# A fused attention and spectral kernel: one weighing of the last attention groups in another bank and behind its phase, one subtraction in two halves, the last image stored in two tiles

## The chip, the cores and the metric

The kernel runs on one core of one Trainium2 chip. A core has TensorE (PE, matrix products into eight banks of accumulator memory), VectorE (DVE), ScalarE (ACT), GpSimd (POOL) and SyncE (SP, which here only issues transfers). The metric is the device time of one execution in microseconds. Before the change three runs took 353.43, 353.55 and 356.92 us; the median is 353.55.

## The reference

Four layers act on x of 4 images, 16 by 16 places, 192 channels, all in float32:

```
x = x + proj(attention(layernorm(x)));  x = x + fc2(gelu(fc1(layernorm(x))))   # layers 0 and 2
x = irfft2(softshrink(mlp(rfft2(x)))) + x                                      # layer 1
x = dht(shrink(mlp(dht(x)))) / size + x                                        # layer 3
```

Attention has 12 heads of 16 channels in windows of 14 by 14 places. 16 is padded to 28, so each image has one full window and three partly filled ones. Each score gets a bias from the row and column distance, then a softmax over the window's keys, and the probabilities weigh the values. Layer 3 is a Hartley transform over images, places and channels, block-diagonal products, and the transform back.

## The kernel before

One program holds an instruction list for each engine, written out by hand. Semaphores order the engines against each other. Every engine works strictly through its own list.

**Attention** (run twice, `attention(l)`, l = 0 and 1) goes through 18 groups, n = 0 to 17. A group is four heads (a slot) of one image's full window or of the edge windows of all images. Groups 14 to 17 are the third slot of images 0 to 3. A group passes through these steps:

- `score` on PE (L910): queries times keys. For groups 2 to 17 it runs in two halves, each half into two banks: part 0 of group n (half-step h = 2n) into banks 0 and 1, part 1 (h = 2n + 1) into banks 2 and 3.
- `take_max` on DVE (L1461): the negated row maximum out of these banks. Then a transpose, and SP moves the maxima by four small transfers (L664) to where `turn` reads them.
- `turn` on PE (L938): the scores once more, keys by queries and less the maximum, into banks 4 to 7. It has two pairs of heads, 8 products each at an image group's full window. Every product is shown in the trace as two records.
- exponentials on ACT (L1294): one for each bank 4 to 7, into a ring of two buffers.
- `weigh` on PE (L957): probabilities times values and ones, 8 products into one bank. `weighed_in(n)` names it: bank 4 for most groups, and 2, 3 and 7 for groups 15, 16 and 17. Bank 4 is also where `turn` of the next group has put scores, so weighing group n in bank 4 waits until the first exponential of group n + 1 has been read.
- `take_weighed` on ACT (L1281): copies the weighed values out, `invert` on DVE (L1484 to L1490) turns and inverts the sums, `divide` on POOL (L723 for the third slot) divides.
- `out_project` on PE (L801): the output product of an image, once its four groups are divided. Image 0 goes to bank 0.

The main loop works three groups at once: `turn` of group n, `score` of groups n + 2 and n + 3, `weigh` of group n - 1. In the loop of n = 15 the last scores (h = 35, group 17) stand between the products of the first pair. Its second pair has no scores beside it: there the order is half of pair 1, the weighing of group 14, the other half of pair 1. ACT follows with exponentials of pair 0, `take_weighed(14)`, exponentials of pair 1. Then come `turn(16)`, `weigh(15)`, `out_project(0)`, `turn(17)`, `weigh(16)`, `out_project(1)`, `weigh(17)`. `turn(16)` waits for all four exponentials of group 15.

**The last stage** (`spectral3`) starts on DVE with sums and differences of the folded images. The difference of images 0 and 1 against 2 and 3 is one instruction over 776 elements (L1574); it releases PE's first two products (`mix` 3 and 2) at once. PE takes mix 3, 2, 0, 1 in turn (L1135), each 4 products.

**The end**: for the images in the order 1, 3, 0, 2, PE transforms back (L1213), 6 products an image for two tiles of 128 places, into one bank. DVE scales and adds x (L1634), and SP stores the image (L670). SP's last wait is for all stores.

```
return {N_GROUPS - 3: 2, N_GROUPS - 2: 3, N_GROUPS - 1: 7}.get(n, 4)      # weighed_in
```

The functions that the change touches:

## Time and profile before

| | |
|---|---|
| median of three runs | 353.55 us (353.43 to 356.92) |
| the profiled execution | 356.79 us |
| its span, first to last instruction | 354.9 us |
| TensorE busy | 338.2 us (95%) |
| VectorE / ScalarE / GpSimd busy | 203.5 / 144.5 / 98.9 us |
| TensorE share of the chain that ended last | 87% |
| mean granted TensorE clock | 0.99 |

The time beside the span is 1.9 us of start and end. The busy shares say who works most over the whole span, but not who is waited for in a given stretch. For that one follows the chain of waits, in order of time, to the places where TensorE itself sat idle, and reads there what ended the idle time. The profiled execution is 3.24 us longer than the median, so its own numbers must be set against its own time.

### The profile page before, as it was taken

The page shows a single profiled execution, that of the slowest core. Times are in us where ns is not written, and L with a number is a line of the kernel's source. Part 1 is how long each engine was busy: PE and PEld are TensorE (multiplying, and loading weights), DVE is VectorE, ACT ScalarE, POOL GpSimd, SP SyncE. Part 2 cuts the span into 40 slices and gives each one's busy share as a digit, 9 for nine tenths or more (in the row PEclk, how much of TensorE's full clock was granted, in tenths as well). Part 3 has the DMA queues.
Part 4 walks back from the last instruction along what each step waited for, and adds up shares of the span by engine and source line. Part 5 has one row for each costly group of instructions (what it writes and reads, how often), then busy time and mean ns, then how long its engine had stood idle before and what let it go on. Part 6 is the DMA issues. An engine that isn't in the chain of part 4 may idle for free.

```text
span 354.9 us, 10541 instructions
## 1 busy us (share of the span) xinstructions
PE 338.2 (95%) x4462; PEld 259.9 (73%) x4462; DVE 203.5 (57%) x483; ACT 144.5 (41%) x322; POOL 98.9 (28%) x186
## 2 busy tenths in 40 slices
PE   5999999999989999999999999999998899999996
PEld 3459698889966447977846878878886643998576
DVE  6455668777766700126765667777785750135472
ACT  2175155555546352023037415555545452202330
POOL 4000507985311029300000050998431204000000
PEclk9699999999999999999999999999999999999999
DMA  6972000000002003010020100000000000000002
GB/s 210 394 252 60 11 10 15 10 5 4 3 17 109 22 1 113 0 66 2 0 90 16 41 3 14 10 9 5 5 4 5 0 0 2 0 2 0 2 0 89
DMA packets 9888, 14.22 MB, mean 40 GB/s; under 512 B 3505, under 2 KB 7441, under 8 KB 9842
## 3 DMA queue, kind: packets, MB, share of 16 engines
q1 hardware_dynamic: 9794, 13.55, 11.8%
q8 instruction: 35, 0.57, 0.7%
q14 instruction: 11, 0.09, 0.1%
q10 hardware_dynamic: 48, 0.00, 0.0%
HBM read 11.30 MB, written 0.79 MB: 34 GB/s over the span
## 4 chain that ended last, share of the span: by engine, by line
PE 87%; DVE 9%; issue 1%; SPq 1%; ACT 1%; DMA 1%; DVEq 0%
PE banks L938 18%; PE banks L910 12%; PE banks L1030 9%; PE banks L1048 9%; PE banks L957 8%; PE banks L867 6%; PE banks L830 4%; PE banks L801 2%; PE banks L790 2%; PE banks L1213 2%; PE banks L1061 2%; PE banks L1108 2%; PE banks L1078 1%; PE banks L1135 1%; PE banks L1161 1%
## 5 line engine op out<-in xcount | busy, mean ns | idle before, releaser
L1294 ACT ACTIVATE arena<-banks 128x392 f32<-128x392 f32 (+2 forms) x144 | 62.5, 486 | 51.2 <-PE banks L938 51.2
L910 PE MATMUL banks<-attention_arena 32*128 32x196 f32 x384 | 49.4, 357 | 0.9 <-ACT v_and_ones L1270 0.4
L938 PE MATMUL banks<-attention_arena 32*128 32x196 f32 x384 | 47.6, 343 | 2.0 <-ACT arena L1294 2.0
L1461 DVE TENSOR_REDUCE negmax<-banks 128x4 f32<-128x784 f32 x40 | 39.0, 975 | 15.8 <-PE banks L910 15.4
L938 PE MATMUL banks<-attention_arena,keys 32*128 32x196 f32 x384 | 44.3, 323 | 0.0
L910 PE MATMUL banks<-keys,attention_arena 32*128 32x196 f32 x384 | 44.0, 323 | 0.0
L938 PEld LDWEIGHTS banks<-attention_arena 32*128 32x128 f32 x384 | 30.1, 183 | 9.0 <-issue 5.8
L1030 PE MATMUL banks<-yT,fc 128*128 128x512 f32 (+1 forms) x96 | 33.3, 607 | 0.3
L1048 PEld LDWEIGHTS banks<-fc,arena 128*128 128x128 f32 x192 | 31.1, 190 | 1.5 <-ACT arena L1308 1.5
L938 PEld LDWEIGHTS banks<-attention_arena,keys 32*128 32x128 f32 x384 | 32.1, 184 | 0.0
L1048 PE MATMUL banks<-fc,arena 128*128 128x192 f32 x192 | 31.7, 327 | 0.0
L910 PEld LDWEIGHTS banks<-keys,attention_arena 32*128 32x128 f32 x384 | 31.5, 184 | 0.0
L1518 DVE TENSOR_TENSOR x_tok<-banks,x_plus_bias 128x384 f32<-128x384 f32 x8 | 4.5, 558 | 46.2 <-PE banks L1048 46.2
L957 PE MATMUL banks<-arena,v_and_ones 128*32 128x196 f32 (+2 forms) x672 | 30.9, 307 | 0.1
L910 PEld LDWEIGHTS banks<-attention_arena 32*128 32x128 f32 x384 | 27.9, 183 | 3.6 <-DVE negmax L1458 1.9
L938 PE MATMUL banks<-edge_rel,edge_keys 32*128 32x112 f32 (+1 forms) x288 | 29.6, 278 | 0.0
L938 PE MATMUL banks<-edge_q,edge_k 32*128 32x112 f32 (+1 forms) x288 | 28.7, 274 | 0.0
L688 POOL COPY edge_rel<-attention_arena 128x112 f32<-128x112 f32 x6 | 1.4, 280 | 91.2 <-DVE attention_arena L1448 91.2
L1030 PEld LDWEIGHTS banks<-yT,fc 128*128 128x128 f32 (+1 forms) x96 | 12.8, 188 | 18.3 <-issue 16.3
L725 POOL TENSOR_TENSOR divided_part<-o_and_sums,inverse_sums 128x196 f32<-128x196 f32 (+2 forms) x24 | 13.1, 546 | 46.5 <-DVE inverse_sums L1490 46.3
L938 PEld LDWEIGHTS banks<-edge_rel,edge_keys 32*128 32x128 f32 x288 | 22.6, 186 | 2.5 <-issue 2.5
L957 PEld LDWEIGHTS banks<-arena,v_and_ones 128*32 128x32 f32 x672 | 16.8, 109 | 10.1 <-ACT arena L1294 6.6
(168 smaller groups left out, 654.6 us busy)
## 6 DMA issues: line engine op xcount, KB each, us to landing
fc<-in_fc SPq DMA_DIRECT2D x2, 768.0 KB, 5.4
qkv<-in_qkv SPq DMA_DIRECT2D x2, 576.0 KB, 4.5
fc<-in_fc SPq DMA_DIRECT2D x2, 576.0 KB, 5.5
attention_arena<-negmaxT SPq DMA_DIRECT2D x68, 1.0 KB
rel<-in_rel SPq DMA_DIRECT2D x2, 448.0 KB, 5.1
x_tok<-in_x SPq DMA_DIRECT2D x4, 192.0 KB, 3.1
inverse<-in_inverse SPq DMA_DIRECT2D x1, 768.0 KB
edge_rel<-negmaxT SPq DMA_DIRECT2D x48, 0.5 KB
```

The source lines that it names most:

```text
L725: pool.tensor_tensor(part, o, shape(m.inverse[:, ring]), ALU.mult).then_inc(s.divided, 1)
L790: last = nc.tensor.transpose(m.bank[bank0 + 2 * g + half][:, 128 * i:128 * (i + 1)], m.xn[:, 4 * g + i, REST * half:REST * half + 128], c[ ...
L801: last = mm(m.bank[out_bank(b)][:, CH * tile:CH * (tile + 1)], m.oT[:, part, at:at + 128], wl["proj"][:, part], start=part == 0, stop=part ...
L830: ins = mm(bank[:, :], wl["qkv"][rows, half, 128 * g:128 * (g + 1)], m.yT[rows, half, 512 * part:512 * (part + 1)], start=not short, stop= ...
L867: ins = mm(bank[row(quad), 192 * n:192 * (n + 1)], wl["rel"][row(quad), 0 if kind == "rel_h" else 1, at % WIN], q[:, :, :, at], start=True ...
L910: ins = mm(o, asking, asked, start=not with_rel, stop=bool(with_rel))
L938: last = mm(m.bank[4 + j][:, cols * tile:cols * (tile + 1)], keys_of(slot, b, j, tile)[with_rel], queries_of(slot, b, j)[with_rel], start= ...
L957: last = mm(m.bank[weighed_in(n)][row(j), 0:cols], values_of(slot, b, j, tile), m.probsT[:, n % P_RING, j, cols * tile:cols * (tile + 1)], ...
L1030: ins = mm(m.bank[j % 8][:, :], wl["fc1"][rows, half, 128 * hid:128 * (hid + 1)], m.yT[rows, half, 512 * g:512 * (g + 1)], start=not short ...
L1048: last = mm(m.bank[4 + b][:, CH * tile:CH * (tile + 1)], m.hidT[:, hid, at:at + 128], wl["fc2"][:, hid], start=hid == 0, stop=hid == HID_T ...
L1294: run(m.probsT[:, n % P_RING, j, 0:cols], m.bank[4 + j][:, 0:cols], ACT.Exp).then_inc(s.probs, 1)
L1461: dve.tensor_reduce(at[:, 4 * part:4 * part + 4].rearrange("k (j a) -> k j a", a=2), m.banks[:, 2 * part:2 * part + 2, 0:2 * MAIN_KEYS].re ...
```

## The change

Four things change.

1. Group 14 is weighed into bank 0 instead of bank 4. So it waits no longer for an exponential of group 15's own bank, but for the maximum of h = 34, the last that reads bank 0. `turn` of groups 16 and 17 waits for one copy-out less (`pv_out` 14 instead of 15), and `out_project(0)`, which uses bank 0, waits for the copy-out of group 14.
2. In the loop of n = 15 (`last_scored`), `weigh(14)` stands behind all of `turn(15)`, and `take_weighed(14)` on ACT behind the exponentials of both pairs. This holds in both attention layers.
3. In `spectral3` the 776-element subtraction becomes two of 388 elements, mix 3 first, each with its own release.
4. The last image's two tiles go to banks 4 and 5, are scaled by two DVE instructions of 192 elements, and are stored by two transfers of half the size.

```diff
@@ -309,3 +309,7 @@
 def weighed_in(n):
-    return {N_GROUPS - 3: 2, N_GROUPS - 2: 3, N_GROUPS - 1: 7}.get(n, 4)
+    return {N_GROUPS - 4: 0, N_GROUPS - 3: 2, N_GROUPS - 2: 3, N_GROUPS - 1: 7}.get(n, 4)
+
+
+def last_scored(n):
+    return n + AHEAD + 1 == N_GROUPS
 
@@ -668,5 +672,10 @@
             for n, b in enumerate(OUT_ORDER):
-                sp.wait_ge(S3.inv.dve, n + 1)
-                sp.dma_start(out_dram[b], m.xb[:, b]).then_inc(stored, 16)
-            sp.wait_ge(stored, 16 * IMAGES)
+                if n < IMAGES - 1:
+                    sp.wait_ge(S3.inv.dve, n + 1)
+                    sp.dma_start(out_dram[b], m.xb[:, b]).then_inc(stored, 16)
+                else:
+                    for tile in range(2):
+                        sp.wait_ge(S3.inv.dve, IMAGES + tile)
+                        sp.dma_start(out_dram[b][:, tile], m.xb[:, b, tile]).then_inc(stored, 16)
+            sp.wait_ge(stored, 16 * (IMAGES + 1))
 
@@ -931,3 +940,3 @@
                     if n >= 2:
-                        pe.wait_ge(s.pv_out, min(n - 1, N_GROUPS - 3))
+                        pe.wait_ge(s.pv_out, min(n - 1, N_GROUPS - 4))
                     at, landed = max_landed(n)
@@ -950,3 +959,3 @@
                     pe.wait_ge(s.probs, 4 * (n + 1))
-                    pe.wait_ge(s.max, 2 * N_GROUPS)
+                    pe.wait_ge(s.max, 2 * N_GROUPS - 1 if weighed_in(n) == 0 else 2 * N_GROUPS)
                 cols, tiles = queries(b), key_tiles(b)
@@ -1001,3 +1010,3 @@
                                 score(l, h + 1, quarter(steps_of(h + 1), q))
-                            if q == 1 and n > 0:
+                            if q == (3 if last_scored(n) else 1) and n > 0:
                                 weigh(l, n - 1)
@@ -1009,3 +1018,3 @@
                             if b == 0:
-                                pe.wait_ge(s.max, 2 * N_GROUPS)
+                                pe.wait_ge(s.pv_out, N_GROUPS - 3)
                             out_project(s, wl, b)
@@ -1131,3 +1140,3 @@
                 for n, mix in enumerate((3, 2, 0, 1)):
-                    pe.wait_ge(S3.mixed, {3: 1, 2: 1, 0: 2, 1: 3}[mix])
+                    pe.wait_ge(S3.mixed, n + 1)
                     for part in range(2):
@@ -1212,5 +1221,7 @@
                                 pe.wait_ge(S3.back.act, 3)
-                            last = mm(m.bank[1 + n][:, CH * tile:CH * (tile + 1)], c["space_back"][:, row, 128 * tile:128 * (tile + 1)], gb,
+                            bank = m.bank[IMAGES + tile if n == IMAGES - 1 else 1 + n]
+                            last = mm(bank[:, CH * tile:CH * (tile + 1)], c["space_back"][:, row, 128 * tile:128 * (tile + 1)], gb,
                                       start=i == 0, stop=i == 2)
-                    last.then_inc(S3.inv.pe, 1)
+                        if tile == 1 or n == IMAGES - 1:
+                            last.then_inc(S3.inv.pe, 1)
 
@@ -1294,3 +1305,3 @@
                             run(m.probsT[:, n % P_RING, j, 0:cols], m.bank[4 + j][:, 0:cols], ACT.Exp).then_inc(s.probs, 1)
-                        if n > 0 and pair == 0:
+                        if n > 0 and pair == last_scored(n):
                             take_weighed(n - 1)
@@ -1573,3 +1584,4 @@
                 dve.wait_ge(S3.folded, FOLDED)
-                dve.tensor_tensor(m.mix[:, 2:4], m.folded[:, 0:2], m.folded[:, 2:4], ALU.subtract).then_inc(S3.mixed, 1)
+                dve.tensor_tensor(m.mix[:, 3], m.folded[:, 1], m.folded[:, 3], ALU.subtract).then_inc(S3.mixed, 1)
+                dve.tensor_tensor(m.mix[:, 2], m.folded[:, 0], m.folded[:, 2], ALU.subtract).then_inc(S3.mixed, 1)
                 dve.tensor_tensor(m.ef[:], m.folded[:, 0:2], m.folded[:, 2:4], ALU.add).then_inc(S3.ef, 1)
@@ -1632,5 +1644,11 @@
                 for n, b in enumerate(OUT_ORDER):
-                    dve.wait_ge(S3.inv.pe, n + 1)
-                    dve.scalar_tensor_tensor(m.xb[:, b], m.bank[1 + n][:, 0:2 * CH].rearrange("k (t c) -> k t c", t=2),
-                                             1.0 / (TOKENS * CH), m.x[:, b], ALU.mult, ALU.add).then_inc(S3.inv.dve, 1)
+                    if n < IMAGES - 1:
+                        dve.wait_ge(S3.inv.pe, n + 1)
+                        dve.scalar_tensor_tensor(m.xb[:, b], m.bank[1 + n][:, 0:2 * CH].rearrange("k (t c) -> k t c", t=2),
+                                                 1.0 / (TOKENS * CH), m.x[:, b], ALU.mult, ALU.add).then_inc(S3.inv.dve, 1)
+                        continue
+                    for tile in range(2):
+                        dve.wait_ge(S3.inv.pe, IMAGES + tile)
+                        dve.scalar_tensor_tensor(m.xb[:, b, tile], m.bank[IMAGES + tile][:, CH * tile:CH * (tile + 1)],
+                                                 1.0 / (TOKENS * CH), m.x[:, b, tile], ALU.mult, ALU.add).then_inc(S3.inv.dve, 1)
```

The lists of the two kernels, first TensorE's, second attention layer. The rows from the second pair of `turn(15)` to the first product of `out_project(0)`. "L957" and "L966" are `weigh`, "L938" and "L947" are `turn`; [waits ...] names the semaphores: `probs` counts exponentials, `max` maxima, `pv_out` copy-outs, `weighed` divisions. Before:

```order
L938 MATMUL banks<-attention_arena 128x196 [waits max_rows1_0,pv_out1,probs1]
L938 MATMUL banks<-attention_arena 128x196
L938 MATMUL banks<-attention_arena,keys 128x196 x2
L957 MATMUL banks<-arena,v_and_ones 32x196 [waits probs1]
L957 MATMUL banks<-arena,v_and_ones 32x196 x7
L938 MATMUL banks<-attention_arena 128x196 x2
L938 MATMUL banks<-attention_arena,keys 128x196 x2
L938 MATMUL banks<-attention_arena 128x196 [waits max_rows1_1,pv_out1,probs1]
```

After:

```order
L947 MATMUL banks<-attention_arena 128x196 [waits max_rows1_0,pv_out1,probs1]
L947 MATMUL banks<-attention_arena 128x196
L947 MATMUL banks<-attention_arena,keys 128x196 x2
L947 MATMUL banks<-attention_arena 128x196 x2
L947 MATMUL banks<-attention_arena,keys 128x196 x2
L966 MATMUL banks<-arena,v_and_ones 32x196 [waits max1,probs1]
L966 MATMUL banks<-arena,v_and_ones 32x196 x7
L947 MATMUL banks<-attention_arena 128x196 [waits max_rows1_1,pv_out1,probs1]
```

The 8 products of the weighing moved behind the second half of `turn(15)`; its wait now names `max` too.

ScalarE's list at the same place, from the exponentials of group 15's first pair to those of group 16's first pair ("L1281" and "L1292" are `take_weighed`, "L1294" and "L1305" the exponentials). Before:

```order
L1294 ACTIVATE arena<-banks 128x392 [waits pv1,turned1_0]
L1294 ACTIVATE arena<-banks 128x392
L1281 ACTIVATE o_and_sums<-banks 128x196 [waits weighed1,pv1]
L1294 ACTIVATE arena<-banks 128x392 [waits turned1_1]
L1294 ACTIVATE arena<-banks 128x392
L1294 ACTIVATE arena<-banks 128x392 [waits pv1,turned1_0]
```

After:

```order
L1305 ACTIVATE arena<-banks 128x392 [waits pv1,turned1_0]
L1305 ACTIVATE arena<-banks 128x392
L1305 ACTIVATE arena<-banks 128x392 [waits turned1_1]
L1305 ACTIVATE arena<-banks 128x392
L1292 ACTIVATE o_and_sums<-banks 128x196 [waits weighed1,pv1]
L1305 ACTIVATE arena<-banks 128x392 [waits pv1,turned1_0]
```

The copy-out moved behind the second pair's exponentials.

## Rows read from the trace of the kernel before

**Rows 1.** Chain of waits, second attention layer: start, duration in us, work, record count

```profile
268.21 0.80 PE banks L957 x16
269.01 0.91 PE banks L938 x8
...
270.89 1.61 PE banks L938 x32
...
273.31 1.50 PE banks L801 x8
```

**Rows 2.** Timeline, same stretch: start, duration, instructions, [idle before <-releaser]

```profile
267.58 0.89 ACT L1294 ACTIVATE arena<-banks 128x392 f32<-128x392 f32 x2 [0.45 <-PE banks L938]
269.16 0.33 ACT L1281 ACTIVATE o_and_sums<-banks 128x196 f32<-128x196 f32 x1 [0.69 <-PE banks L957]
269.95 0.89 ACT L1294 ACTIVATE arena<-banks 128x392 f32<-128x392 f32 x2 [0.46 <-PE banks L938]
270.89 0.61 PE L938 MATMUL banks<-attention_arena 32*128 32x196 f32 x8 [1.01 <-ACT arena L1294]
```

**Rows 3.** The same timeline, VectorE, GpSimd and SyncE

```profile
266.33 0.97 DVE L1461 TENSOR_REDUCE negmax<-banks 128x4 f32<-128x784 f32 x1 [0.16 <-PE banks L910]
268.99 2.20 SPq L664 DMA_DIRECT2D attention_arena<-negmaxT  x4
273.81 0.41 DVE L1484 STREAM_TRANSPOSE o_turned<-o_and_sums 128x224 f32<-128x224 f32 x1 [2.91 <-ACT o_and_sums L1281]
274.99 0.61 POOL L723 TENSOR_TENSOR attention_arena<-o_and_sums,inverse_sums 128x196 f32<-128x196 f32 x1 [3.40 <-DVE inverse_sums L1490]
279.50 0.46 PEld L801 LDWEIGHTS banks<-proj,attention_arena 128*128 128x128 f32 x3 [0.43 <-POOL attention_arena L723]
278.83 0.61 POOL L723 TENSOR_TENSOR attention_arena<-o_and_sums,inverse_sums 128x196 f32<-128x196 f32 x1 [3.23 <-DVE inverse_sums L1490]
```

**Rows 4.** Timeline, first attention layer

```profile
104.41 0.61 PE L938 MATMUL banks<-attention_arena 32*128 32x196 f32 x8 [1.01 <-ACT arena L1294]
108.22 0.41 DVE L1490 STREAM_TRANSPOSE inverse_sums<-recip 128x224 f32<-128x224 f32 x1 [0.23 <-DVE recip L1486]
```

**Rows 5.** Timeline, start of the last stage, VectorE and TensorE

```profile
319.78 0.97 DVE L1574 TENSOR_TENSOR arena<-attention_arena 128x776 f32<-128x776 f32 x1
320.66 0.96 DVE L1575 TENSOR_TENSOR arena<-attention_arena 128x776 f32<-128x776 f32 x1
321.65 0.56 DVE L1577 TENSOR_TENSOR arena<-arena 128x388 f32<-128x388 f32 x1
322.14 0.56 DVE L1578 TENSOR_TENSOR arena<-arena 128x388 f32<-128x388 f32 x1
323.98 0.30 DVE L1591 TENSOR_TENSOR arena<-banks,arena 97x144 f32<-97x144 f32 x1
320.80 4.16 PE L1135 MATMUL banks<-space_cas,arena 128*97 128x144 f32 x32 [0.64 <-DVE arena L1574]
```

**Rows 6.** Timeline, end: the last scaling and its store

```profile
351.91 0.56 DVE L1634 SCALAR_TENSOR_TENSOR x_plus_bias<-banks,x_tok 128x384 f32<-128x384 f32 x1 [1.39 <-PE banks L1213]
352.50 0.37 SPq L670 DMA_DIRECT2D out<-x_plus_bias  x1
```

**Rows 7.** Page, issues: KB each, us to landing

```profile
out<-x_plus_bias SPq DMA_DIRECT2D x4, 192.0 KB, 2.0
```

**Rows 8.** Stretches: busy time of five engines, granted clock, transfer share, GB/s

```profile
353.30:353.40 0.10, 0.00 (x0) 0.00 (x0) 0.00 (x0) 0.00 (x0) 0.00 (x0) 1.00 0.11 38
354.00:354.10 0.10, 0.00 (x0) 0.00 (x0) 0.00 (x0) 0.00 (x0) 0.00 (x0) 1.00 0.31 92
9.00:10.00 1.00, 0.75 (x1) 0.50 (x2) 0.97 (x7) 0.00 (x0) 0.00 (x0) 0.50 1.05 358
```

**Rows 9.** Chain of waits, first projection of the kernel

```profile
9.25 5.46 PE banks L830 x6
...
15.92 4.94 PE banks L830 x14
```

## The prediction

> **What bounds the kernel now.** I read the chain of waits first, in order of time. TensorE carries 87% of it, so an instruction of another engine is worth time only where TensorE stands still beside it. The change touches four places, and TensorE stands still at three of them.
>
> In each attention layer the chain leaves TensorE once between groups 15 and 16. In the second layer it runs: `weigh(14)` at 268.21 for 0.80, the second half of `turn(15)` at 269.01 for 0.91, then ScalarE, then `turn(16)` at 270.89 [rows 1]. The timeline shows why: the exponentials of group 15's second pair start at 269.95, 0.03 us after that half, and take 0.89, while TensorE is idle for 1.01 us and is released by them [rows 2]. So the weighing stands in front of the work that ScalarE waits for, and the time behind it is empty. The first layer has the same 1.01 us [rows 4]. At the start of the last stage TensorE idles 0.64 us for one subtraction of 0.97 us [rows 5]. At the end nothing runs beside the last scaling, its store and the landing [rows 6, 7].
>
> **The change part by part.**
>
> *The weighing behind `turn(15)`, twice.* Nothing is added or removed; 0.80 us of TensorE's work moves behind the last products of `turn(15)`. These end at 269.92 - 0.80 = 269.12. ScalarE is free then (its first pair ended at 267.58 + 0.89 = 268.47), and has no copy-out in front any more. It runs from 269.15 to 270.04. `turn(16)` started 0.05 after the exponentials and does so again, at 270.09 instead of 270.89: **0.80 us**. The weighing ends at 269.92 and lies in the gap, of which some 0.2 us is left. Its new wait, the maximum of h = 34, was done at 266.33 + 0.97 = 267.30 [rows 3], so bank 0 is free.
>
> What gets later is the copy-out of group 14: from 269.16 to 270.04. Behind it hang VectorE's inversion, GpSimd's division and `out_project(0)`. The same steps for group 15 take from 273.81 to the end of the division at 274.99 + 0.61 = 275.60, so 1.79 us. The copy takes 0.33 and VectorE starts some 0.03 behind it: 270.40 + 1.79 = 272.19. From a division to TensorE the row of `out_project(2)` shows 279.50 - 279.44 = 0.06 us. So `out_project(0)` is released at 272.25 [rows 2, 3]. TensorE reaches it at 273.31 - 0.80 = 272.51. That is 0.26 us of slack. In the first layer one inversion stood 0.23 us longer between two of its own steps [rows 4]; there the slack is 0.03. I cost this at nothing, and name it as the tightest place.
>
> SyncE's queue isn't touched here, but the small transfers of the maxima now have less time. The last four issues end at 268.99 + 2.20 = 271.19. Even with the 2.0 us of the 192 KB store they land at 273.2, and `turn(17)` needs them at 272.51 + 1.50 = 274.01 [rows 3, 7]. The copy-out wait of `turn` 16 and 17 goes away, but was no row's releaser. Everything behind is released by TensorE, so it moves with it. Two layers: 1.60 us. Bounds: at most the whole idle, 1.01 each; at least 0.4 each, if the division is late.
>
> *The subtraction in halves.* One of 776 elements took 0.97; one of 388 takes 0.56, and the next of a pair starts 0.49 behind the first [rows 5]. TensorE starts 0.05 behind 319.78 + 0.56, at 320.39 instead of 320.80: **0.41 us**. The second half is done at 320.83, needed at 321.43 (each mix takes 4.16/4 = 1.04). VectorE's later work starts 2 x 0.49 - 0.88 = 0.10 later. So mix 0 is ready at 321.65 + 0.56 + 0.10 + 0.05 = 322.36 and needed at 320.39 + 2.08 = 322.47. The last input of the channel products (L1591) is ready at 323.98 + 0.30 + 0.15 = 324.43 and needed at 324.55. Both are covered by TensorE's own products, by only 0.11 us. Without that cover up to 0.1 us is given back; bounds 0.30 to 0.41.
>
> *The last image by tiles.* TensorE ends when it did. The last scaling shrinks from 384 to 192 columns. Between 0.30 for 144 and 0.56 for 384 elements [rows 5, 6], 192 take 0.30 + 48 x 0.26/240 = 0.35: 0.21 us less. The store lands 2.0 us after its issue; its bytes move from about 353.39 to 354.03, 0.64 us [rows 7, 8], of which half goes: 0.32. The first tile's store is issued a microsecond earlier, so its 0.37 of SyncE lies before the second tile is ready. **0.53 us.** For the landing the bounds are 0 (it is all fixed) and 1.0 (it is all proportional); I take 0.32, since the bytes' own time is what the rows show.
>
> The Trainium skill (DMA: Bandwidth & Descriptors, Anatomy of one DMA) fits about 2.0 us plus bytes/436e3, on the GpSimd path. By it the half store saves 0.23 instead of 0.32, and the sum falls by 0.09. Its whole for 192 KB would be 2.45, and the row has 2.0, so the fit is high here; I stay with the rows.
>
> The fourth edit, banks 4 and 5 for the two tiles, costs nothing: bank 5 was last read before the first image's products. The sum is 1.60 + 0.41 + 0.53 = 2.54 us.
>
> **Against which time.** The profiled execution took 356.79, the median 353.55. The difference has a place: from 9 to 15 us TensorE's granted clock is 0.50, its level of 1.2 GHz, after a stretch with idle time before it [rows 8]. Six records of the first projection take 5.46 there, against 14 in 4.94 later at 2.4 GHz, which is 0.353 each [rows 9]. That is 5.46 - 2.12 = 3.34 us, against 3.24 between profile and median. So I take the sum off both: 354.25 for an execution with this fall, 351.0 for one without.
>
> **The rivals.**
>
> *The division becomes the wait.* For it: slacks of 0.26 and 0.03. Against it: eight such divisions of one length. If two steps stand 0.23 longer, as one did, the layers lose 0.20 and 0.43: 351.0 + 0.6 = 351.6, and to 352.2 at the bounds. It decides from 0.26 us on.
>
> *The median falls on executions with the slow stretch.* This is the one that ends above the time before. The place is the first projection, the price 3.3 us, and it decides when more than half of the timed runs have it: 351.0 + 3.3 = 354.3, slower than 353.55 by 0.2%. For it: of four executions shown two have such a time (356.79, 356.92). Against it: the change leaves everything before 100 us as it was, and the median before was free of it. The Trainium skill (TensorE: Matmul & The Clock Gate, What's actually happening) says that the point at which the clock rises differs from run to run of one kernel. The two groups of times agree with that.
>
> *Nothing is won in attention*, because the exponentials were held by something else than the products. The rows name only the products. It would leave 0.94 us: 352.6.
>
> **How the numbers follow.** Forecast 60%, late division 12%, slow stretch 24%, nothing in attention 2%, other 2%. The predicted time is 351.0. The forecast's own range adds up the bounds: a gain of 1.3 gives 352.2, one of 3.1 (most of the idle time and 0.9 at the end) 350.4. The slow stretch must be in, or a quarter is left out, so the range is 350.5 to 354.5. A measurement of this kernel can tell about 1% from no change, which is 3.5 us. Faster by more needs a gain of 3.5, beyond the bounds unless the two kernels' medians fall on different sides of the slow stretch: 6%. Slower by more needs both the stretch and something unforeseen: 2%. Within: 92%.
>
> **What would show it.** `turn(16)` should start 0.2 us behind the end of `weigh(14)`, in both layers, and the 1.01 us of idle time be gone. No wait on GpSimd before `out_project(0)`, or one below 0.1. TensorE's idle before L1135's successor near 0.23, with no new one between the mixes. A last scaling of 0.35 and a landing near 1.7. Wrong would be: an idle TensorE before `out_project(0)` of over 0.3, a wait on VectorE before mix 0 or the channel products, a landing of 2.0 still, or a clock of 0.50 anywhere behind 16 us.

## The result

Eighteen runs of each kernel gave a median of 351.93 us (350.38 to 353.88) for the changed one and 355.23 us (353.34 to 357.27) for the one before. The ratio of the two kernels, which is that of their mean times (352.05 and 355.00), is 0.9917, with a 95% interval of 0.9892 to 0.9942. That is 2.95 us less, with an interval of 2.1 to 3.8; the two medians are 3.30 us apart. Runs that took over 1.5% more than the fastest of the same kernel are left out of the medians, ranges and ratios of this text; among these thirty-six there is none. The prediction was 351.0, in a range of 350.5 to 354.5, with "within 1%" at 92%, and a sum of 2.54 us off. The measured median lies in the range. The three runs that the prediction started from had a median of 353.55; the kernel before is 1.7 us slower than that in the longer series, so the fall of 2.95 is what can be compared with the 2.54, and the median cannot be taken off 353.55.

The changed kernel's page:

```profile
PE 338.1 (96%) x4462; PEld 260.3 (74%) x4462; DVE 204.1 (58%) x485; ACT 144.6 (41%) x322; POOL 99.1 (28%) x186
```

TensorE does the same work (338.1 against 338.2 us) in a span of 351.3 us, which is 3.6 us shorter. The rest of this section finds those 3.6 us.

**The attention groups.** The chain of waits of the changed kernel, second attention layer, as [rows 1]:

```profile
265.82 1.35 PE banks L947 x16
...
267.59 0.50 ACT arena L1305
268.09 0.04 issue
268.13 1.61 PE banks L947 x32
269.74 0.80 PE banks L966 x16
270.54 1.50 PE banks L810 x8
```

The weighing stood as a piece of 0.80 us between two pieces of `turn(15)`. It has left the chain, and the last 16 records of `turn(15)` are one piece of 1.35 us. Before, they were two, of 0.66 and 0.91 us. The first layer shows both:

```profile
101.06 0.66 PE banks L938 x8
101.73 0.80 PE banks L957 x16
102.53 0.91 PE banks L938 x8
```

The timeline of the same stretch, as [rows 2, 3]:

```profile
267.02 0.21 DVE L1487 STREAM_TRANSPOSE negmaxT<-negmax 128x32 f32<-128x32 f32 x1
267.19 0.89 ACT L1305 ACTIVATE arena<-banks 128x392 f32<-128x392 f32 x2 [0.45 <-PE banks L947]
268.10 0.33 ACT L1292 ACTIVATE o_and_sums<-banks 128x196 f32<-128x196 f32 x1
268.13 0.61 PE L947 MATMUL banks<-attention_arena 32*128 32x196 f32 x8 [0.18 <-ACT arena L1305]
269.64 0.61 POOL L732 TENSOR_TENSOR attention_arena<-o_and_sums,inverse_sums 128x196 f32<-128x196 f32 x1 [0.89 <-DVE inverse_sums L1501]
270.47 0.62 PEld L810 LDWEIGHTS banks<-proj,attention_arena 128*128 128x128 f32 x4 [0.31 <-issue]
```

TensorE's idle time before `turn(16)` fell from 1.01 to 0.18 us. The transpose of the last maximum (L1487) hangs on the last scores, ahead of the edit, so it is a good mark to measure from: from it to `turn(16)` are 268.13 - 267.02 = 1.11 us. Its row before:

```profile
268.75 0.21 DVE L1476 STREAM_TRANSPOSE negmaxT<-negmax 128x32 f32<-128x32 f32 x1
```

There it was 270.89 - 268.75 = 2.14. Each layer gained **1.03 us**, not 0.80; the first layer shows the same 1.11 and 2.14.

**The start of the last stage**, timeline and then chain of waits of the changed kernel, as [rows 5]:

```profile
317.02 0.56 DVE L1585 TENSOR_TENSOR arena<-attention_arena 128x388 f32<-128x388 f32 x1
317.50 0.56 DVE L1586 TENSOR_TENSOR arena<-attention_arena 128x388 f32<-128x388 f32 x1
...
321.30 0.30 DVE L1603 TENSOR_TENSOR arena<-banks,arena 97x144 f32<-97x144 f32 x1
317.64 4.16 PE L1144 MATMUL banks<-space_cas,arena 128*97 128x144 f32 x32 [0.24 <-DVE arena L1585]
```

```profile
321.80 4.00 PE banks L1154 x16
```

TensorE waits 0.24 instead of 0.64 us, which is a gain of 0.40. But the next stage (L1154, the channel products) takes 4.00 us. Before it took 3.88:

```profile
324.96 3.88 PE banks L1145 x16
```

So 0.11 to 0.12 us was given back.

**The end**, timeline and issues of the changed kernel, as [rows 6, 7]:

```profile
348.27 1.32 SPq L679 DMA_DIRECT2D out<-x_plus_bias  x2
348.86 0.36 DVE L1652 SCALAR_TENSOR_TENSOR x_plus_bias<-banks,x_tok 128x192 f32<-128x192 f32 x1 [0.62 <-PE banks L1223]
```

```profile
out<-x_plus_bias SPq DMA_DIRECT2D x2, 96.0 KB, 1.6
```

The last scaling takes 0.36 instead of 0.56, the landing 1.6 instead of 2.0. The landings are rounded to 0.1, and so are the spans on the page. The traces hold the spans to the thousandth: 354.878 and 351.277 us. From the first record of the back transform (343.71 and 340.66) to the end that is 11.17 and 10.62: the end gained **0.55 us**, of which 0.20 are the scaling and 0.35 what lies behind it.

The pieces add up: 2 x 1.03 + 0.40 - 0.11 + 0.55 = 2.90 us. The other 0.70 us between the two spans lie before 24 us, where nothing was changed (last part of the experiments): the next stage begins at 24.55 and 23.85. So the 3.60 us are complete. The 2.95 us of the eighteen runs agree with the 2.90, but with an interval of 2.1 to 3.8 they would agree with 2.54 as well.

### The profile page after: what moved, and what is told of

Read it like the earlier page. It is cut to its first block, busy times and chain, and to the rows that moved or that the text cites. A ratio compares the mean times of both kernels' runs of the same rounds, so it can differ in the third digit from the quotient of the medians.

```text
span 351.3 us, 10546 instructions
## 1 busy us (share of the span) xinstructions
PE 338.1 (96%) x4462; PEld 260.3 (74%) x4462; DVE 204.1 (58%) x485; ACT 144.6 (41%) x322; POOL 99.1 (28%) x186
## 4 chain that ended last, share of the span: by engine, by line
PE 87%; DVE 8%; issue 1%; DMA 1%; ACT 1%; SPq 1%; DVEq 0%
PE banks L947 18%; PE banks L919 12%; PE banks L1039 9%; PE banks L1057 9%; PE banks L966 7%; PE banks L876 6%; PE banks L839 4%; PE banks L799 3%; PE banks L810 2%; PE banks L1223 2%; PE banks L1070 2%; PE banks L1117 2%; PE banks L1087 1%; PE banks L1144 1%; PE banks L1170 1%
## 5 line engine op out<-in xcount | busy, mean ns | idle before, releaser
L1305 ACT ACTIVATE arena<-banks 128x392 f32<-128x392 f32 (+2 forms) x144 | 62.5, 486 | 50.5 <-PE banks L947 50.5
L947 PE MATMUL banks<-attention_arena 32*128 32x196 f32 x384 | 47.2, 341 | 0.5 <-ACT arena L1305 0.4
L947 PE MATMUL banks<-attention_arena,keys 32*128 32x196 f32 x384 | 44.3, 323 | 0.0
L947 PEld LDWEIGHTS banks<-attention_arena 32*128 32x128 f32 x384 | 30.2, 183 | 6.8 <-issue 5.1
L947 PEld LDWEIGHTS banks<-attention_arena,keys 32*128 32x128 f32 x384 | 32.1, 184 | 0.0
L966 PE MATMUL banks<-arena,v_and_ones 128*32 128x196 f32 (+2 forms) x672 | 30.9, 307 | 0.1
L947 PE MATMUL banks<-edge_rel,edge_keys 32*128 32x112 f32 (+1 forms) x288 | 29.6, 278 | 0.0
L947 PE MATMUL banks<-edge_q,edge_k 32*128 32x112 f32 (+1 forms) x288 | 28.7, 274 | 0.0
L947 PEld LDWEIGHTS banks<-edge_rel,edge_keys 32*128 32x128 f32 x288 | 22.6, 186 | 2.5 <-issue 2.5
L966 PEld LDWEIGHTS banks<-arena,v_and_ones 128*32 128x32 f32 x672 | 16.8, 109 | 10.1 <-ACT arena L1305 6.2
```

The costliest lines, as they stand in the source:

```text
L947: last = mm(m.bank[4 + j][:, cols * tile:cols * (tile + 1)], keys_of(slot, b, j, tile)[with_rel], queries_of(slot, b, j)[with_rel], start= ...
L966: last = mm(m.bank[weighed_in(n)][row(j), 0:cols], values_of(slot, b, j, tile), m.probsT[:, n % P_RING, j, cols * tile:cols * (tile + 1)], ...
L1305: run(m.probsT[:, n % P_RING, j, 0:cols], m.bank[4 + j][:, 0:cols], ACT.Exp).then_inc(s.probs, 1)
```

## The experiments

I had two theories for the 0.23 us that each attention layer gained above the forecast. S, switching: TensorE loses time whenever it goes from `turn`'s products to a weighing and back. W, waiting: the weighing itself stood waiting for the exponential that frees bank 4. The mark for all kernels is again the transpose of the last maximum:

| kernel | mark to `turn(16)`, layers 1 and 2, us | idle before `turn(16)` | `turn(16)` to `out_project(0)` |
|---|---|---|---|
| before | 2.14, 2.14 | 1.01 | 2.34, 2.35 |
| changed | 1.11, 1.11 | 0.18 | 2.34, 2.34 |
| e1_attention | 1.11, 1.11 | 0.18 | 2.34, 2.34 |
| e4_bank_only | 2.14, 2.14 | 1.01 | 2.34, 2.35 |
| e5_moved_bank4 | 1.50, 1.51 | 0.58 | 2.35, 2.34 |
| e6_act_order | 2.23, 2.23 | 1.31 | 2.35, 3.96 |
| e7_split | 1.11, 1.11 | 0.18, 0.17 | 2.55, 2.56 |
| e9_pool_late | 1.11, 1.11 | 0.18 | 2.55, 2.55 |

The differences are of start times in each kernel's own timeline; the last column goes to the first record of `out_project(0)`. Where a kernel was run once, its whole time is given but not argued from, since single runs of one kernel differ by some 3 us.

**e1_attention** (354.03 us): the kernel before with the attention edits alone.

```diff
-                            if q == 1 and n > 0:
+                            if q == (3 if last_scored(n) else 1) and n > 0:
...
-                        if n > 0 and pair == 0:
+                        if n > 0 and pair == last_scored(n):
```

> The kernel before with the attention edits alone (bank 0, the weighing of group 14 behind all of turn(15), the copy-out behind both pairs). Forecast's sizes: turn(16) starts 0.80 us earlier in each layer and the span is 1.6 us shorter between the same two places. The changed kernel's trace has 1.03 us in each layer. Theory S (switching): a TensorE that goes from turn to weigh and back loses about 0.1 us each way, and the order saves that too: 1.03 us each, 2.06 in both, and the start of the last stage still idles 0.64 us. Theory W (waiting): the 0.23 us above the forecast were a wait of the weighing for the exponential of bank 4.

Measured: 1.03 us in each layer, and 0.64 us of idle time left at the start of the last stage. So the attention edits are worth 2.06 us by themselves.

**e4_bank_only** (355.97 us): the kernel before with group 14 in bank 0, but nothing moved.

```diff
-    return {N_GROUPS - 3: 2, N_GROUPS - 2: 3, N_GROUPS - 1: 7}.get(n, 4)
+    return {N_GROUPS - 4: 0, N_GROUPS - 3: 2, N_GROUPS - 2: 3, N_GROUPS - 1: 7}.get(n, 4)
```

> The kernel before with group 14 weighed in bank 0, but at its old place (in the middle of turn(15)'s second pair) and the copy-out at its old place. The wait for the exponential is gone, the switches stay. Theory W: turn(16) starts 0.2 us earlier in each layer (idle before it still about 1.0). Theory S: nothing moves, below 0.05 us.

Its chain, first layer, has the same pieces as before:

```profile
100.27 0.66 PE banks L938 x8
100.94 0.80 PE banks L957 x16
101.74 0.91 PE banks L938 x8
...
103.61 1.61 PE banks L938 x32
```

Nothing moved, to the hundredth. The wait for the exponential cost nothing: W falls.

**e7_split** (353.85 us): the changed kernel with the weighing of group 15 put into the middle of `turn(16)`.

```diff
-                        turn(l, n, None, range(steps))
-                        weigh(l, n - 1)
+                        if n == N_GROUPS - 2:
+                            turn(l, n, None, range(2))
+                            weigh(l, n - 1)
+                            turn(l, n, None, range(2, steps))
...
```

> The changed kernel with the weighing of group 15 put into the middle of turn(16), in both layers: the same products, with two more changes between turn and weigh. From the start of turn(16) to the start of out_project(0) the changed kernel takes 2.41 us. Theory S: 2.41 + 0.1 to 0.23 here. Without a cost of switching: 2.41.

The timeline of its first layer shows where it goes:

```profile
101.88 0.61 PE L947 MATMUL banks<-attention_arena 32*128 32x196 f32 x8 [0.18 <-ACT arena L1310]
102.31 0.51 PE L947 MATMUL banks<-attention_arena,keys 32*128 32x196 f32 x8
102.75 0.88 PE L966 MATMUL banks<-arena,v_and_ones 128*32 128x196 f32 x16
103.56 0.61 PE L947 MATMUL banks<-attention_arena 32*128 32x196 f32 x8
104.00 0.51 PE L947 MATMUL banks<-attention_arena,keys 32*128 32x196 f32 x8
```

From the first of eight records to the first of the next eight are 0.44 us where `turn` begins anew (101.88 to 102.31, 103.56 to 104.00) and where the weighing follows (102.31 to 102.75). The changed kernel's unbroken `turn(16)` has one such step at its start, one at its end, and two of 0.33 between. The same products, in the same number, took 0.21 us longer (2.55 against 2.34), with no wait in between. S holds: about 0.1 us each way, 0.21 for a weighing put into a `turn`. In the changed kernel both switches of `weigh(14)` lie in the time in which TensorE waits anyway. The kernel before shows them too: 0.66 + 0.91 us in two pieces against 1.35 in one are 0.22, which is the missing 0.23 but for rounding. The two kinds of product differ in shape, operands and bank; which of these costs the time was not tested.

**e5_moved_bank4** (354.93 us): the weighing and its copy-out moved as in the change, but still in bank 4. Its edit is that of e1_attention, shown above, without the new entry in `weighed_in` and the waits that go with bank 0.

> The kernel before with the weighing of group 14 and its copy-out moved, but still in bank 4. turn(16) writes bank 4 and must wait for the copy-out, which now runs behind the exponentials: exponentials end + 0.33 us. Both theories: turn(16) starts 0.35 us later than in the changed kernel, idle before it about 0.5 us instead of 0.18; so the bank is worth 0.35 us of the 1.03. A rival: the bank is worth nothing, since TensorE waits for the exponentials anyway: idle 0.18.

Its timeline, second layer:

```profile
267.69 0.89 ACT L1298 ACTIVATE arena<-banks 128x392 f32<-128x392 f32 x2 [0.45 <-PE banks L942]
268.60 0.33 ACT L1285 ACTIVATE o_and_sums<-banks 128x196 f32<-128x196 f32 x1
269.03 0.45 PE L942 MATMUL banks<-attention_arena 32*128 32x196 f32 x4 [0.58 <-ACT arena L1298]
```

`turn(16)` starts 0.10 us behind the end of the copy-out (268.93), where in the changed kernel it starts 0.03 us behind that copy's start. That is 0.39 to 0.40 us later than in the changed kernel, a little more than the 0.35 expected. The move alone gives 0.63 us of the 1.03 and the bank the other 0.40, though the bank alone gives nothing. The releaser that the row names (L1298) is not the one that ended the wait, since it was done at 268.58; the copy-out was.

**e6_act_order** (357.73 us): the changed kernel with ScalarE's copy-out back between the pairs.

```diff
-                        if n > 0 and pair == last_scored(n):
+                        if n > 0 and pair == 0:
```

> The changed kernel with the copy-out of group 14 back between the two pairs' exponentials, while the weighing stays behind turn(15). ScalarE then waits for the weighing (0.80 us behind the end of turn(15)) and copies 0.33 us before it starts the exponentials: turn(16) starts 0.80 + 0.07 + 0.27 = 1.1 us later than in the changed kernel, idle before it 1.3 us, so that nothing of the attention gain is left (0.1 us slower than before in each layer). If ScalarE's order did not matter, idle stays at 0.18.

ScalarE waits 1.35 us for the weighing, and the exponentials start behind the copy-out. First layer:

```profile
103.43 0.33 ACT L1292 ACTIVATE o_and_sums<-banks 128x196 f32<-128x196 f32 x1 [1.35 <-PE banks L966]
103.66 0.88 ACT L1305 ACTIVATE arena<-banks 128x392 f32<-128x392 f32 x2
104.59 0.61 PE L947 MATMUL banks<-attention_arena 32*128 32x196 f32 x8 [1.31 <-ACT arena L1305]
```

`turn(16)` is 1.12 us later than in the changed kernel and 0.09 later than before, as expected. In the second layer something came on top: from `turn(16)` to `out_project(0)` it took 3.96 instead of 2.35 us. The stretches of that kernel (busy time of PE, PEld, DVE, ACT and POOL, then granted clock, transfer share, GB/s):

```profile
270.00:271.00 1.00, 0.00 (x0) 0.00 (x0) 0.71 (x3) 0.99 (x3) 0.45 (x1) 1.00 0.05 10
272.00:273.00 1.00, 1.00 (x20) 1.00 (x16) 0.00 (x0) 0.00 (x0) 0.15 (x1) 0.50 0.00 1
```

The clock went from 2.4 to 1.2 GHz at 271.3, 0.1 us after TensorE had gone on behind its 1.31 us of idle time, was back at 2.4 GHz by 275, and the fall cost 1.6 us. In the first layer the same 1.31 us left it at 2.4 GHz. This is one fall in one execution, so that the idle time caused it is not shown. Its mean granted clock is 0.986. The kernel before has three executions with that clock too, with 1.01 us of idle time at both places: they took 358.48, 358.89 and 359.15 us. No trace shows where theirs was low.

**e2_halves** (354.93 us): the kernel before with the subtraction in halves alone.

```diff
-                dve.tensor_tensor(m.mix[:, 2:4], m.folded[:, 0:2], m.folded[:, 2:4], ALU.subtract).then_inc(S3.mixed, 1)
+                dve.tensor_tensor(m.mix[:, 3], m.folded[:, 1], m.folded[:, 3], ALU.subtract).then_inc(S3.mixed, 1)
+                dve.tensor_tensor(m.mix[:, 2], m.folded[:, 0], m.folded[:, 2], ALU.subtract).then_inc(S3.mixed, 1)
```

> The kernel before with the subtraction of the last stage in two halves alone. Forecast: the mixes start 0.41 us earlier and everything behind does. The changed kernel's trace has 0.40 there but gives back 0.11 at the channel products (L1154 starts its weight load 0.12 us late). If the halves cause that: the products of the channel stage (chain of waits) take 4.00 instead of 3.88 here too, and 0.29 us is left. If it came from the other edits: 3.88.

Its chain:

```profile
318.26 4.16 PE banks L1135 x32
322.42 4.00 PE banks L1145 x16
```

The idle time is 0.24, and the channel products take 4.00: the halves bring 0.40 and give back 0.12. The end of this execution took 0.68 us longer than before, all of it behind the last scaling, where nothing was changed (see e3_tiles).

**e8_flip_later** (351.65 us): the changed kernel with VectorE's copy of the flipped image 3 behind the four operations that make the channel products' input.

```diff
-                for b in range(1, IMAGES, 2):
+                def take_flipped(b):
...
+                take_flipped(1)
...
                 dve.tensor_tensor(m.z[0:FOLD, 1, 3], g[:, 1], h[:, 1], ALU.subtract).then_inc(S3.fwd.dve, 1)
+                take_flipped(3)
```

> The changed kernel with VectorE's second copy of the flipped images (image 3) moved behind the four operations that make the channel products' input. That input is then ready 0.4 us earlier. Theory: the 0.11 us was the weight load of the first channel product waiting for VectorE; the channel stage in the chain of waits goes back from 4.00 to 3.88, with no new wait for the copy, which the fourth product needs 2.9 us later. Rival: the 0.11 is the products' own; 4.00 stays.

Its chain, and the weight loads of the stage:

```profile
320.50 3.88 PE banks L1154 x16
```

```profile
320.21 0.80 PEld L1154 LDWEIGHTS banks<-arena,chan_fwd 97*128 97x128 f32 x4
```

The 3.88 is back. The first weight load starts 0.29 us ahead of the products' piece in the chain. In the changed kernel it starts at 321.65, only 0.15 ahead of its piece and 0.05 behind the end of VectorE's last input (321.60):

```profile
321.65 3.69 PEld L1154 LDWEIGHTS banks<-arena,chan_fwd 97*128 97x128 f32 x16
```

**e9_pool_late** (352.32 us): one more copy on GpSimd, never read, ahead of group 14's division.

```diff
+                        if n == N_GROUPS - 4:
+                            pool.tensor_copy(m.part[:, ring], m.o[:, ring, 0:MAIN_KEYS])
```

> The changed kernel with one more copy of 196 elements on GpSimd ahead of the division of group 14 (about 0.35 us by the 112-element copies' 0.28). The copy's result isn't used. In the changed kernel's trace the division ends 0.16 to 0.22 us before out_project(0) needs it. If that is the slack: TensorE idles 0.15 to 0.3 us before out_project(0) in each layer. If the slack is larger than shown: no idle.

GpSimd and TensorE's weight load, first layer:

```profile
103.07 0.35 POOL L733 COPY divided_part<-o_and_sums 128x196 f32<-128x196 f32 x1 [0.87 <-DVE inverse_sums L1503]
103.38 0.61 POOL L734 TENSOR_TENSOR attention_arena<-o_and_sums,inverse_sums 128x196 f32<-128x196 f32 x1
104.10 0.19 PEld L812 LDWEIGHTS banks<-proj,attention_arena 128*128 128x128 f32 x1 [0.49 <-issue]
```

The division starts 1.80 us behind `turn(16)` instead of 1.51, so 0.29 later, and the first product of `out_project(0)` 0.21 later, in both layers. The slack of the changed kernel is thus 0.08 us. From the division's end (103.99) to the weight load are 0.11 us. The row calls the wait "issue" and does not name GpSimd.

**e3_tiles** (355.31 us): the kernel before with the last image by tiles alone.

```diff
-                dve.wait_ge(S3.inv.pe, n + 1)
...
+                    for tile in range(2):
+                        dve.wait_ge(S3.inv.pe, IMAGES + tile)
```

> The kernel before with the last image by tiles alone. Forecast: last scaling 0.35 instead of 0.56, landing 2.0 less 0.32. The changed kernel's trace has 0.36 and 1.6. Theory (bytes and part of the rest): from the end of the last product to the end of the span 0.60 us less than before, and nothing else moves. If the 1.6 came from other traffic in that run: a landing of 1.7 or more.

From the first record of the back transform to the end of the span it takes 353.517 - 342.89 = 10.63 us, against 11.17 before: 0.54 less, where 0.60 was expected. The last scaling is 0.36, the landing of the 96 KB stores 1.6. The idle times at the other places are those of before.

Every other trace either has this edit or lacks it, so each measures the piece once more. The nine with two tiles take 10.60 to 10.63 us. Of the five with the whole image four take 11.17 or 11.18, and e2_halves 11.85. So the 0.55 us are large against the spread of all traces but that one, in which the last store landed 0.7 us late for a reason that no trace shows.

**The start: e10_fill, e11_fill_warm, e12_best.** The forecast held that the 3.24 us between the first profile and the first median were a stretch at 1.2 GHz that other executions do not have. The chain of the changed kernel speaks against it:

```profile
9.48 4.86 PE banks L839 x6
...
15.22 4.94 PE banks L839 x14
```

The six records still take 4.86 us, where [rows 9] have 5.46. In this profile the granted clock is given as 1.00 all the while:

```profile
12.00:13.00 1.00, 1.00 (x2) 0.34 (x1) 0.22 (x1) 0.00 (x0) 0.00 (x0) 1.00 1.01 361
```

But the records there start 0.85 us apart, twice the 0.43 that the same products have at 180 us in the kernel before. So they run at the lower level, and the clock column does not tell it at this place: the trace's first clock record lies at 13.6 us, and the view prints 1.00 where it has none. All eleven traces of the two kernels and of e1 to e9 have such a stretch. The six records take from 4.23 to 5.49 us, and the next stage begins anywhere from 22.54 to 24.77 us.

The stretch comes in two kinds. The eight transposes ahead of the idle time tell them apart, here in the changed kernel and in the kernel before:

```profile
6.52 1.97 PE L799 MATMUL banks<-ident,normed 128*128 128x128 f32 x8 [0.74 <-DMA slot_cols<-in_slot_cols]
6.29 1.09 PE L790 MATMUL banks<-ident,normed 128*128 128x128 f32 x8 [0.82 <-DVE normed L1409]
```

In four traces (the changed kernel, e1, e4, e5) they take 1.97 us, in all others 1.09 to 1.22. In the four, TensorE was thus at the lower level already, ahead of the idle time, and did not fall in it. In the others it had risen and fell. To test whether the idle time sets it, idle products fill that time:

```diff
                     turn_norm(s.ln[0], 0, 0)
+                    for _ in range(2):
+                        mm(m.bank[7][:, 0:2 * MAIN_KEYS], m.probsT[:, 0, 0, 0:128], m.probsT[:, 0, 0, :], start=True, stop=True)
```

These are products whose result is never read. e10_fill has two. e11_fill_warm has three, four warm-ups instead of three, and e8's edit; e12_best three, three warm-ups and e8's edit.

> The changed kernel with two idle products of 392 columns (the warm-up's own, into bank 7, never read) between the first transposes and the first projection, where TensorE stands idle for 1 to 2 us and after which the clock is at 1.2 GHz until 12 to 15 us. If the idle time is what lets the clock fall, the stretch at 1.2 GHz ends sooner: the first six records of the projection take 2.1 to 3.5 us instead of 4.3 to 5.5, and the time is 1 to 3 us below the changed kernel's 351.9. If the clock goes by what happened before these transposes or not by this idle time: they take the same, and the start is up to 1 us later, since the idle products take 1.3 us each at 1.2 GHz.

> The changed kernel with four instead of three warm-up products, three idle products between the first transposes and the projection, and the second flipped copy behind the channel products' input. TensorE is then never idle for more than 0.3 us from 1.5 us on. If idle time is the cause of the slow stretch: as above and more surely, 349 to 351 us with a smaller spread than 350.4 to 353.9. If not: 352 to 353, later by the products' own time.

> The changed kernel with three idle products between the first transposes and the projection (warm-ups left at three) and the second flipped copy moved behind the channel products' input. By the theory that idle time lets the clock fall: first six records of the projection near 2.6 us, channel stage 3.88, a time of 350.5 to 351.5 with a spread of at most 2 us, about 1.5% below the kernel before. If the two earlier filled kernels' times were luck: 352 and a spread of 3.5 us, like the changed kernel.

| kernel | runs | median (range), us | before on the same chip | ratio, 95% interval | six records | next stage at |
|---|---|---|---|---|---|---|
| e10_fill | 4 | 351.16 (350.68 to 352.34) | 356.12 (353.28 to 357.46) | 0.9846 [0.9786, 0.9907] | 2.81 | 22.23 |
| e11_fill_warm | 4 | 351.14 (350.50 to 351.65) | the same | 0.9839 [0.9790, 0.9888] | 2.57 | 22.13 |
| e12_best | 12 | 350.95 (350.38 to 352.79) | 353.41 (352.90 to 356.99) | 0.9921 [0.9890, 0.9952] | 2.58 | 21.92 |

The chain of e12_best:

```profile
6.64 1.22 PE banks L799 x8
7.86 1.98 PE banks L981 x6
9.83 2.58 PE banks L839 x6
```

The six records run 0.43 us apart, and the next stage begins ahead of all eleven unfilled traces: in these three executions the projection has no stretch at 1.2 GHz. In e10 TensorE still stood idle for 1.12 us right before the projection, so it was not needed to fill every gap. In all three the transposes take at most 1.22 us, so all three are of the kind that had risen in time. What filling does to the other kind is not shown.

In the time this shows only in part, and some expectations for it were missed: e12 is 0.8% below the kernel before, not 1.5%, and spreads over 2.4 us, not 2; e10 and e11 lie just outside their ranges. The lowest times of the changed kernel and of e12 are equal (350.38), and e12's slowest is 1.1 us below the changed kernel's. But its ratio to the kernel before is the same within the intervals. e10 and e11 have a lower ratio with four runs each, on a chip on which the kernel before had a median of 356.12. Of e12's twelve runs eight took 350.38 to 351.24 us and four 352.32 to 352.79, with none between; no trace of a late one was taken. What makes these late is not known; a TensorE that starts low, as in the four traces above, could be it. That the median of a filled kernel is below that of the changed one is not shown: the two were never timed side by side.

## Why the prediction was right, and where it was not

**The place and the mechanism** held: the idle time before `turn(16)` was the exponentials' wait, and fell from 1.01 to 0.18 us against a forecast of 0.2.

**The attention term** was 1.60 and is 2.06 us. The step "0.80 us of TensorE's work moves behind the last products" took the weighing for its own duration. What moved was also the two switches, 0.23 in each layer. The trace of the kernel before holds them: the eight records behind the weighing take 0.91 us [rows 1], and the eight ahead of it 0.66, while the 16 in one piece take 1.35. I took the duration of the piece that moves and did not ask what the pieces beside it would be without it.

**The division's slack** was called the tightest place, with 0.26 and 0.03 us. It did not become the wait. It is 0.08 us in both layers by e9_pool_late, so the first layer's 0.03 was too careful (the extra 0.23 us of its row did not recur), the second's 0.26 too generous. So the gain escaped this rival by 0.08 us. I had taken TensorE's arrival from the chain (2.41 us behind `turn(16)`), while its weight load stands there at 2.34 and needs the division 0.11 us earlier, not 0.06.

**The halves**: 0.41 forecast, 0.40 found at the first mix. The cover of "only 0.11 us" over the channel products was not enough, and 0.12 was given back; the net 0.29 is just below the bound of 0.30. A wait on VectorE before the channel products was one of the prediction's own signs of being wrong, and it came. The failing step is the same as for the division: the input had to be there for the weight load, not for the first product. Before, the load stood 0.28 us ahead of the end of the mixes. VectorE's later work came 0.10 later and TensorE's need 0.40 earlier. The mixes themselves were covered, as forecast.

**The end**: 0.53 forecast, 0.55 found, 0.54 by e3_tiles. The scaling was right (0.35 and 0.36). What lies behind it fell by 0.35 against 0.32, half the bytes' own time. The fit of the Trainium skill (DMA: Bandwidth & Descriptors, Anatomy of one DMA), with 0.23, was further off. The rows of landings, 2.0 and 1.6, are rounded and would give 0.4.

**Which time.** The step that failed is "I take the sum off both". There are not two groups of executions, with and without the slow stretch. The stretch is in every unfilled trace, with a varying end, and the times lie in several groups. For the changed kernel the six runs with a mean granted clock of 0.995 took 351.82 to 351.97 us and the two at 0.990 took 353.60 and 353.88. Of the ten at 0.999 or 1.000 six took 350.38 to 351.40 and four 353.07 to 353.34, among them the profiled one, whose clock records begin behind its slow stretch. The kernel before goes from 353.34 to 357.27 in steps of at most 0.9 us. The forecast's 351.0 goes with the lowest executions (350.38 against 353.34 before, 2.96 us apart), and the median of 351.93 lies above it, by 0.9 us. That the number came so near is in part luck: the prediction started from a median 1.7 us too low for the longer series, and its sum was 0.4 too small for the mean difference, 0.8 for that of the medians.

The rival of the slow stretch named the right place; the measured median would also lie in the forecast's own range of 350.4 to 352.2. Its price of 3.3 us for a median was too high, since the kernel before pays it too. It was also worked out wrongly: the 14 records in 4.94 us (0.353 each) are mostly products with 64-row weights, and the six have 128 rows. The same six take 2.58 us at 2.4 GHz in e12, not 2.12, so the stretch cost the projection 5.46 - 2.58 = 2.88 us, not 3.34. The transposes behind it, 1.21 us in the chain of the kernel before against 0.87 in e12, are another 0.34.

The errors in the sum, +0.46 in attention, -0.13 for the halves and +0.02 at the end, make the 0.36 us between 2.54 and the 2.90 found in the traces.

What stays open: what sets the length of the stretch at 1.2 GHz when nothing is filled in, why TensorE had not risen at all before it in four of eleven traces, and what makes some executions of e12 late.

## What to carry to other kernels

If an engine waits idle for a second engine, look in its list ahead of the wait for work that the second engine doesn't need, move it into the idle time, and move the second engine's matching step too: e6 shows that one move without the other is worse than none (by 0.09 us in its first layer), and e5 that the moved work needs a bank that the next products don't wait for (0.40 of the 1.03 us). Count with such work the switches on both sides of it. Measure TensorE's slack to its weight load, not to its product; twice here that was 0.1 us, and once it decided.

## What the runs showed of the hardware

- Going from products with 32-row weights to products with 128-row weights and 32 columns, and back, cost TensorE 0.21 us a pair (e7_split: 2.55 against 2.34 us for the same products).
- In one layer of e6_act_order the clock fell to 1.2 GHz right behind 1.31 us of idle TensorE, for some 3 us, which cost 1.6 us; in the other layer the same idle time left it at 2.4 GHz. The cause is not shown.
- At the start of a program the granted clock of the profile read 1.00 while products started 0.85 us apart that start 0.43 us apart later. There the distance of equal products tells the level better than the column.
- A product was late by 0.12 us because its weight load had to wait for VectorE, whose input was done at 321.60, although TensorE was at work on other products until 321.80 (the stage took 4.00 us; 3.88 with the input earlier, in e8_flip_later).
- Halving the bytes of the last store (192 to 96 KB) took 0.35 us off the time behind the last scaling, 2.41 against 2.06. In the one trace of e2_halves the 192 KB store landed another 0.68 us later.
- A row's releaser can be wrong or missing when two engines end close together: in e5 it named the exponentials, in e9 "issue" stood for GpSimd.
